# Turns 2 to 30 of a four-layer graph network kernel as a runtime loop on each engine

## The reference

```
h = max(layernorm(x), 0)          # ahead of every layer
layer 0:  s1 = h @ W1.T; s2 = h @ W2.T               # W = adj, 256 wide
          e[i,j] = sum_e a[e] * leaky(s1[i,e] + s2[j,e] + b_lin[e]) + adj[i,j]
          x += sigmoid(softmax(e) @ h)
layer 1:  edge network with elu, sigmoid edges under a mask, two dense maps
layer 2:  attention, tanh-bounded logits, masked by adj
layer 3:  5 steps of a gated recurrent update, messages adj @ h
```

## Time and profile before

| | |
|---|---|
| median of 3 runs | 5742.77 us |
| profiled execution | 5747.33 us |
| its span | 5745.5 us, 123558 instructions |
| busy PE / ACT / POOL / DVE | 98% / 92% / 87% / 86% |
| granted TensorE clock | 0.995 |

### The profile page before, as it was taken

One profiled execution on the slowest core, in us unless ns is written; L12 is line 12 of the kernel. 1 busy time (PEld: TensorE's weight loads), 2 busy tenths in 40 slices (PEclk: granted clock), 3 DMA queues, 4 the chain that ended last, 5 costly groups with the idle time before them and its releaser, 6 DMA issues.

```text
span 5745.5 us, 123558 instructions
## 1 busy us (share of the span) xinstructions
PE 5620.1 (98%) x40844; PEld 2179.6 (38%) x40844; DVE 4965.1 (86%) x9389; ACT 5260.0 (92%) x12857; POOL 4988.5 (87%) x10246
## 2 busy tenths in 40 slices
PE   8999999999999999999999999999999999999996
PEld 2333333333333333333333333333333333333334
DVE  9998888889888888888898888888888888889883
ACT  8999999999999999999999999999999999999983
POOL 8989888889898898898898888988989888889880
PEclk9999999999999999999999999999999999999998
DMA  0000000000000000000000000000000000000000
GB/s 14 3 4 7 7 6 3 7 6 7 7 2 7 6 7 7 6 3 7 6 7 6 3 7 6 7 7 6 3 6 7 7 6 3 7 6 7 7 5 6
DMA packets 44275, 34.45 MB, mean 6 GB/s; under 512 B 4736, under 2 KB 39552, under 8 KB 43648
## 3 DMA queue, kind: packets, MB, share of 16 engines
q1 hardware_dynamic: 43648, 26.56, 1.5%
HBM read 9.77 MB, written 8.39 MB: 3 GB/s over the span
## 4 chain that ended last, share of the span: by engine, by line
PE 81%; DVE 9%; ACT 5%; POOL 3%; issue 2%; DMA 0%; SPq 0%; POOLq 0%; DVEq 0%
PE S L991 49%; PE R L939 14%; DVE ring L597 5%; PE W L939 5%; PE S L939 4%; ACT ring L794 4%; PE R L1128 2%; PE PA L939 2%; POOL ring L487 2%; PE R L1136 1%; PE PB L939 1%; DVE ring L592 1%; POOL rstd L461 1%; PE PB L1016 1%; DVE st L650 0%
## 5 line engine op out<-in xcount | busy, mean ns | idle before, releaser
L487 POOL TENSOR_SCALAR ring<-W,U 128x256 f32<-128x256 f32 x9536 | 4681.5, 518 | 138.8 <-PE S L991 131.2
L794 ACT ACTIVATE ring<-W,U_minus 128x256 f32<-128x256 f32 x10336 | 4241.1, 506 | 10.7 <-issue 5.7
L991 PE MATMUL S<-ring,a_window 128*32 128x512 f32 x32768 | 3709.3, 596 | 76.2 <-POOL ring L487 44.3
L597 DVE TENSOR_TENSOR ring<-U,W 128x512 f32<-128x512 f32 (+1 forms) x3808 | 3186.0, 861 | 0.2 <-PE S L991 0.2
L991 PEld LDWEIGHTS S<-ring,a_window 128*32 128x32 f32 x32768 | 977.9, 110 | 2513.1 <-issue 2395.1
L592 DVE TENSOR_TENSOR ring<-U,W 128x256 f32<-128x256 f32 x2592 | 1039.8, 406 | 0.0
L458 POOL TENSOR_TENSOR minus_mean<-mv,minus_one 128x4 f32<-128x4 f32 (+1 forms) x160 | 31.8, 199 | 515.6 <-DVE mv L657 494.2
L939 PE MATMUL R<-mT,W 128*128 128x512 f32 (+1 forms) x640 | 332.8, 602 | 2.1 <-ACT mT L898 2.1
L939 PE MATMUL R<-AT,h 128*128 128x256 f32 x1260 | 308.8, 388 | 2.7 <-ACT h L910 2.1
L730 DVE SCALAR_TENSOR_TENSOR rh<-tr,h3T 128x512 f32<-128x512 f32 (+1 forms) x165 | 125.0, 758 | 176.2 <-ACT tr L901 172.2
L939 PEld LDWEIGHTS R<-AT,h 128*128 128x128 f32 x1260 | 229.0, 192 | 79.0 <-ACT h L910 27.9
(11 more groups left out here) (173 smaller groups left out, 4070.5 us busy)
## 6 DMA issues: line engine op xcount, KB each, us to landing
X<-in_x SPq DMA_DIRECT2D x64, 128.0 KB, 2.1
X_held<-X SPq DMA_DIRECT2D x32, 256.0 KB, 2.3
out<-OUT SPq DMA_DIRECT2D x64, 128.0 KB, 2.0
raw<-in_L_gnn_w_w SPq DMA_DIRECT2D x3, 128.0 KB, 2.3
A<-in_adj SPq DMA_DIRECT2D x1, 256.0 KB, 2.7
Wn<-in_L_gnn_Wn SPq DMA_DIRECT2D x1, 128.0 KB, 2.5
Wm<-in_L_gnn_Wm SPq DMA_DIRECT2D x1, 128.0 KB, 2.5
rawu<-in_L_gnn_u_w SPq DMA_DIRECT2D x2, 64.0 KB, 2.4
```

What stands on the lines that cost most here:

```text
L487: last = gp.tensor_scalar(ring[:, place, g, half * N:(half + 1) * N], W[:, y, c], LARGEST, U[:, y, c, i:i + 1], ALU.min, ALU.max)
L597: piece = dve.tensor_tensor(ring[:, place, g:g + groups].rearrange("p g (h j) -> p g h j", h=NB), u.unsqueeze(3).to_broadcast([P, groups, ...
L794: last = act.activation(ring[:, place, g, half * N:(half + 1) * N], W[:, y, c], ACT.Relu, bias=U_minus[:, y, c, i:i + 1])
L991: last = pe.matmul(S[y][g * ROWS:(g + 1) * ROWS, :], a_window[:, c, ROWS - 1 - row:2 * ROWS - 1 - row], ring[:, place, g], start=False, st ...
```

## The change

`run_turns` still writes turns 0 and 1 out, then puts turns 2 to 30 into a runtime loop on that engine (`it` from 0 to 28), and writes turns 31, 32 and 33 out. The wait values and the DRAM offsets inside the loop become expressions of `it`. `Fori` keeps a counter in a register of the engine; after the body it adds one, compares with the end and branches back. The loops of the engines are independent: no barrier is added.

```diff
     def run_turns(eng, body):
-        for m in range(PAIRS + 2):
+        for m in range(2):
+            body(Turn(m=m))
+        with eng.Fori(0, PAIRS - 3) as it:
+            body(Turn(it=it))
+        for m in range(PAIRS - 1, PAIRS + 2):
             body(Turn(m=m))
```

## The result

The loop makes the kernel slower: 5806.69 us median of 5 runs (5804.33 to 5818.76) against 5742.84 us for the kernel before, a ratio of 1.011 with a 95% interval of 1.0098 to 1.0124. That is 64 us, 2.3 us for each of the 28 taken back-edges. The forecast was 5746 us, with 5790 as its upper end.

The account below looks back on a forecast made before the run. The prediction took PE to bound the kernel: a 4.0 us fetch less 2.0 us queued and 1.88 us of waiting left 0.12 us per edge, 3.4 us over 28, added to 5742.77 for 5746 us; range 5732 to 5790.

Parts of the forecast that it names:

- What bounds the kernel; the place to look.: PE bounds it, busy 4887.8 of 4930.6 us in steady turns; look at the turn boundary, where the branch goes.
- The fetch, 2.2 to 4.8 us with 4.0 taken, against 2.0 us of queued work.: At PE's back-edge, the missing instruction block stops the sequencer 4.0 us; less queued work, L983 starts 2.0 us late.
- The other engines cost nothing.: At the edges of POOL, DVE, ACT and SP, queued work or standing covers the stop: no term.
- Register work, 0.: Within the turn, waits comparing with registers are hidden by the 2.0 us of PE's queue: taken as 0.
- The 1.88 us of waiting that PE would have done anyway.: In a turn's first lots PE waits three times for POOL, 1.88 us in all, which swallows a delay at the boundary.
- "Less 1.88 of waiting ...: 0.12 us per edge.": At PE's edge, the 2.0 us late start less 1.88 us of waiting leaves 0.12 us, 3.4 us over 28 edges.
- a rival with a chance of 0.08: A second fetch miss in PE's same edge, another 2.1 to 4.3 us each, about 5830 us; chance 0.08.
- the late wait for DVE in 10 of 28 turns: Later in some turns PE stands 0.83 us for DVE; about 10 of 28 turns are long, by 1.07 us.
- rival 6: PE's late wait for DVE comes in all turns: 18 us more, 5764 us with the edge; chance 0.06.
- a gain: PE, starting its lots later, never meets the late wait for DVE: 10 us less, 5733 us; chance 0.06.

Follow-up runs that it names:

- cut at lot 82: The changed kernel with PE's loop running from lot 82 of a turn to lot 81 of the next, no hint: 5744.79 us, ratio 1.0009.
- head at slot 0: The changed kernel with PE's loop beginning at the first slot of an instruction fetch block: 5768.75 us, ratio 1.0041.
- slot 200: The changed kernel with PE's loop beginning 56 instructions from the end of a 256-instruction fetch block: 5769.34 us, ratio 1.0051.

## Why the prediction was wrong

Its steps, one by one.

*What bounds the kernel; the place to look.* Right. PE is the bound, the loss is at L987 and in the lots just behind it, and it is PE's alone.

*The fetch, 2.2 to 4.8 us with 4.0 taken, against 2.0 us of queued work.* Right, and closely: 3.8 us in the edge shown, 2.0 us of idle in each of the 28, and no idle where the queue held more (cut at lot 82).

*The other engines cost nothing.* Right in result and reason: POOL's stop shortened its wait for L661. The run without PE's loop is at 1.0001.

*Register work, 0.* Right, as far as can be told: 1.0003 (up to 1.0013) with all of it and a hint.

*The 1.88 us of waiting that PE would have done anyway.* Right: with the head at slot 0 and the clock at full, PE reaches the transpose 9.95 - 8.07 = 1.88 us sooner than in the kernel before, without a wait for POOL.

*"Less 1.88 of waiting ...: 0.12 us per edge."* This step failed. The sum had one fetch per edge, and there are two. I had the second as a rival with a chance of 0.08, taken from 30 of 256 slots as if the head's slot were drawn by lot. The slot is fixed by the code ahead of the loop and is the same in all 28 edges, so the price falls due at each edge or at none. The price that I gave it, 2.1 to 4.3 us, was too high: it is 1.78 us, of which 0.54 is shown as idle in the start above. The first gap has already used up the 1.88 us of waiting, so nothing is left to take the second, and all of it is lost. In turns at full clock the change takes 178.44 us and the loop with its head at slot 0 takes 176.30: 2.1 us per edge, 60 us of 28 edges. Placement took only 38 us away, because without the second fetch the clock costs more.

*The clock.* Left out altogether, and wrong to leave out. I had seen the granted clock at 1.00 around waits of 0.57 us and asked no further. A 2 us gap is followed in some turns by 3.4 us at 1.2 GHz. In the changed kernel this adds little: its 10 turns with such a stretch are 0.3 us longer than the other 18, 3 us in all. With the head at slot 0, where nothing else covers it, it is 1.0 us per edge, 28 us in the profiled execution of 5771 us. The Trainium skill ("TensorE: Matmul & The Clock Gate", Part 1: The HAM clock gate (the "warmup" mystery)) says that this gate goes by how busy the array has been, with 1.2 GHz for idle and 2.4 GHz for busy. The trace agrees with the two levels. By that section of the Trainium skill the clock falls only after longer idling than in these gaps of 1.7 to 2.4 us. With the head at slot 0 it fell behind 16 of the 28, and the measurement decides.

The terms for the changed kernel, per edge at full clock: 2.2 for the first gap, 1.8 for the second, less 1.88, is 2.1 us. PE's late waits for DVE add 0.3 (below). The 18 turns at full clock are 178.44 - 176.09 = 2.35 us longer. With the other 10 the steady turns went from 176.1 to 5000.3 / 28 = 178.6 us in the window below, 2.5 us.

```profile
487.80:5488.10 5000.30, 4917.99 (x35674) 1942.19 (x35674) 4348.14 (x8168) 4599.69 (x11226) 4376.91 (x8960) 1.00 0.02 6
```

The medians differ by 2.3 per edge. What lies between, 5 us in all, is less than what single executions differ by: turns 0 and 1, the same code in both, took 14 us less in this execution than in the profiled one of before, which had 17.1 us at 1.2 GHz in them against 3.4.

One more thing that I had as rivals, the late wait for DVE in 10 of 28 turns, moved towards rival 6 and not towards a gain: in the steady turns PE waits for DVE's L601 22 times for 14.4 us, against 10 times for 7.5. With 0.21 more for each wait that is 0.3 us per edge. It also comes with no loss: with all engines but PE in loops it is there 28 times, at a ratio of 1.0001. What moves it wasn't tested.

The Trainium skill's rule that a taken branch out of the loaded pages stalls for a fetch ("Runtime: NRT & Kernel Launch", Instruction fetch mechanics) agrees with the trace on PE, DVE, ACT and POOL; SP went on after 0.2 us. Whether the stop costs time is another matter: on all engines but PE it was free, and on PE nearly so once the cut was moved (1.0009).

## What to carry to other kernels

The back-edge of a long hand-written loop stopped the sequencers of the compute engines for 2.4 to 4.0 us here. Its price on the engine that bounds the kernel is that stop, less the work queued on the engine, less the waits that the engine would have done anyway; each of the two can be spent only once, so a second stop behind the first is paid in full. Hint the back-edge of the bounding engine, or cut the loop where its queue is longest: both brought this loop within 0.1% of the kernel before. When a price depends on where code lies in a fetch block, it is not a chance to be spread over edges but one draw for all of them: count the slot, or set it.

## What the runs showed of the hardware

- A taken back-edge on PE took 3.3 to 3.9 us in the branch itself (median 3.5), and mostly 0.44 us with a hint on all engines (1.7 at the most); with the hint on PE alone the median is 1.25. The row of the changed kernel is below; its least value, 83 ns, is the last pass, where the branch is not taken:

```profile
L211 PEldq COMPARE_BRANCH  x29: 83/3530/3885, 483.7 to 5485.3; - x29
```

- On DVE, ACT and POOL the branch's record is 45 to 68 ns and the stop comes behind it: over the 28 edges 2.9 to 3.8 us to the next instruction on DVE, 2.4 to 2.8 on ACT, 2.6 to 3.2 on POOL. A list of long instructions doesn't show it. SP went on after 0.2 us.
- The block behind the loop's head arrives late as well: with 17 instructions to the block's end PE waited, with 56 it didn't.
- A stop in the middle of four matmuls on 32 columns each cost 1.8 us for 0.54 us of idle shown.
- Gaps of 1.7 to 2.4 us on PE were followed by 3.4 us at 1.2 GHz in 16 of 28 turns with the head at slot 0 and 14 of 28 at slot 200, and in 10 of 28 in the changed kernel. It never showed in the looped turns of the runs without the gap. The gaps before a fall and before none overlap in length (1.76 to 2.35 and 1.70 to 2.11 us with slot 0), so their length alone doesn't tell which it will be.
